# Three transformer layers behind a rotation: layers written out, w_up and the value columns converted elsewhere, setup transfers rearranged

## The chip, the cores and the metric

The kernel runs on one core of one Trainium2 chip. The metric is the device time of one execution in microseconds (us); less is better. All work is in fp32 accuracy: a matmul operand is split into a high part (fp32r) and a low part (the fp32 rest), and three products stand for one.

## The reference

Sixteen samples (B) of 256 tokens (T) with 288 channels (C). Layer 0 rotates each sample in a 64-dimensional subspace: it takes U from a QR factorisation of P and a rotation R = expm(A(cond)) per sample. Three layers follow, each with its own weights, modulated by the condition:

```python
z = einsum('btn,nd->btd', x, U)
x = x + einsum('btd,nd->btn', einsum('btd,bde->bte', z, R) - z, U)
for each of three layers:
    shift_a, scale_a, gate_a, shift_f, scale_f, gate_f = split(silu(cond) @ W_ada + b_ada, 6)
    h = layernorm(x) * (1 + scale_a) + shift_a
    q, k, v = h @ W_qkv + b_qkv            # 16 heads of 18
    x = x + gate_a * (softmax(q @ k.T / sqrt(18)) @ v @ W_proj + b_proj)
    h = layernorm(x) * (1 + scale_f) + shift_f
    x = x + gate_f * (gelu(h @ W_fc1 + b_fc1) @ W_fc2 + b_fc2)   # hidden size 1152
```

## The kernel before

`prepare` is the setup: rotation, modulation, and the first sample's queries, keys and values. The block of `layers` follows it behind a barrier of all engines. There each engine runs its own program, written out by hand in order and tied to the others by semaphores only. A program is a `prologue`, 48 half steps (`half_step(l, b)`: layer l, sample b, `it` = 16 l + b) and an `epilogue`. A half step works on three samples at once: attention of sample `it`, projection and MLP of sample `it - 1`, and queries, keys, values and first scores of `it + 1`.

TensorE goes, in a half step, through: projection of `it - 1` (two halves), the transposes of the maxima, then qk tile groups 0, 1, 2 of `it + 1` with shifted score units 0 to 2 between them, unit 3, the MLP transposes, unit 4, weighted values, units 5 and 6, values of `it + 1`, unit 7, `up` 0 to 4 with values between, score units of `it + 1` and `down`. Score units 5 to 7 need the b transfers of `stacks`.

`whole_run` (line 1492) sets the loops: half step (0, 0), then a loop over l = 0, 1 in the instruction stream that holds half step 1, an inner loop over b = 2 to 13, half steps 14, 15 and (l + 1, 0), and behind it a second copy for the last layer. So the code of a half step exists 10 times, and one jump leads back from (1, 0) to half step 1.

Weights come from DRAM in pieces and are converted: ACT or DVE copies the high part, POOL or DVE subtracts it to get the low part.
- w_up has two raw pieces of 128 x 1152 and three of 384 columns through staging. ACT makes the high parts (`high_weights`), POOL the low ones (`low_weights`, L1645): the first raw piece at the end of half step 0, the rest at the start of half step 1.
- w_in's query and key columns are converted by DVE in half step 14 (B-2), its value columns by DVE in half step 15 (B-1), behind the attention norm (`convert_weights`, L2264 and L2269). TensorE's `values` wait for them (`weights_ready`).
- `mlp_low` (POOL, L1636), `mlp_high` (DVE, L2242 to 2245), x_hat (DVE, L2230) and qk_low (DVE, L2253) are in every half step.

On ACT, `negate_maxima` (L1819) turns the transposed maxima into neg_max; ACT and SP each carry half of it into q_stack, and shifted unit 0 waits for both. `load_sums` waits for the store of the softmax sums and stands between gelu 0 and gelu 1.

SP issues most transfers in order: in the setup twelve query transfers (`query_stack`), then in the block of layers ten stores of rotated samples (L1538), a wait for the first keys, a signal to TensorE for score unit 5 (L1540), a wait for the stores (L1542), and `negated_maxima(0)`. In a half step: w_down's load (half step 1), x_mid, gates, x_in, `stacks` with 24 transfers, and in half step 0 the load of w_up's raw pieces behind them.

## Time and profile before

| what | value |
|---|---|
| median of 3 runs | 2068.33 us (2067.29 to 2071.01) |
| profiled execution | 2067.53 us, span 2065.8 us |
| TensorE busy (matmuls) | 1956.7 us, 95% |
| DVE, ACT, POOL busy | 1204.7, 1122.2, 1005.8 us (58, 54, 49%) |
| granted clock of TensorE, mean | 0.977 |
| start of the block of layers, first scores | 155.4, 156.8 us |
| mean half step from 300 us on | about 38 to 39 us |

The difference between the profiled execution's time and its span, 1.7 us, lies around the span. A granted clock of 1.0 is 2.4 GHz and 0.5 is 1.2 GHz. PE is TensorE's matmuls, PEld its weight loads. In a timeline row the bracket gives the idle time before the instruction and what ended it; "issue" means that the engine waited for nothing that the profile shows. In a row of waits the three numbers are the total, how many there were, and the longest.

### The profile page before, as it was taken

What the parts mean: (1) busy time and instruction counts of PE and PEld (TensorE: products, weight loads), DVE (VectorE), ACT (ScalarE), POOL (GpSimd) and SP (SyncE); (2) the same over time, 40 slices, a digit from 0 to 9 for tenths busy, and PEclk for the clock granted to TensorE, in tenths of its full rate; (3) what the DMA queues carried; (4) which work ended last, traced back from release to release, by engine and by line L of the source; (5) the groups of instructions that cost most, each with busy time, mean ns of one, the idle gap of its engine ahead of it and who ended that gap; (6) DMA issues with size and microseconds to landing.
All of it is one profiled execution on the core that took longest, in us unless ns stands there. A gap on an engine that the chain in (4) does not pass through costs nothing. (4 is left out here: it accounts for less than half of the span.)

```text
span 2065.8 us, 49808 instructions
## 1 busy us (share of the span) xinstructions
PE 1956.7 (95%) x16599; PEld 1748.2 (85%) x16599; DVE 1204.7 (58%) x2656; ACT 1122.2 (54%) x1929; POOL 1005.8 (49%) x1034
## 2 busy tenths in 40 slices
PE   6786999999999989899999999999899999999996
PEld 3554889989989979798999999988798999999986
DVE  7884655655546565655654655674665554654641
ACT  5333466465565556456556566455546556556452
POOL 1003645545545436554555544645564554544534
PEclk9997999999999999999999999999999999999998
DMA  8625433233333333433333333233433333333220
GB/s 220 136 72 162 118 107 98 83 102 91 92 95 87 99 89 112 142 92 94 89 95 98 81 105 98 83 103 95 138 82 103 91 92 95 87 101 99 76 80 26
DMA packets 138403, 207.01 MB, mean 100 GB/s; under 512 B 35688, under 2 KB 95686, under 8 KB 137254
## 3 DMA queue, kind: packets, MB, share of 16 engines
q1 hardware_dynamic: 110226, 168.27, 29.6%
q10 hardware_dynamic: 25460, 29.78, 5.2%
q0 software_dynamic: 2624, 7.77, 1.4%
q8 instruction: 53, 0.87, 0.2%
q14 instruction: 40, 0.33, 0.1%
HBM read 99.18 MB, written 20.82 MB: 58 GB/s over the span
## 5 line engine op out<-in xcount | busy, mean ns | idle before, releaser
L2277 DVE TENSOR_REDUCE maxima<-scores 128x4 f32<-128x1024 f32 x384 | 460.8, 1223 | 177.6 <-PE scores L2032 170.9
L1636 POOL TENSOR_TENSOR hidden<-g_full,hidden 128x512 fp32r<-128x512 f32 (+1 forms) x240 | 280.9, 1178 | 354.1 <-ACT hidden L1872 353.0
L1829 ACT ACTIVATE probs<-scores 128x1024 f32<-128x1024 f32 x384 | 383.3, 1027 | 94.6 <-PE pv_ps L2069 55.2
L2094 PE MATMUL mlp_ps<-h_mlp,w_up 128*128 128x256 f32 (+1 forms) x3024 | 406.3, 287 | 6.9 <-POOL h_mlp L1636 4.0
L2094 PEld LDWEIGHTS mlp_ps<-h_mlp,w_up 128*128 128x128 f32 (+1 forms) x3024 | 379.4, 191 | 36.4 <-issue 20.0
L1957 PE MATMUL mlp_ps<-w_down,hidden 128*128 128x288 f32 x2592 | 390.8, 296 | 0.0
L1957 PEld LDWEIGHTS mlp_ps<-w_down,hidden 128*128 128x128 f32 x2592 | 370.0, 189 | 18.6
L2032 PE MATMUL scores<-k_stack,q_stack 108*128 108x512 f32 x768 | 240.9, 406 | 17.5 <-DMA k_stack<-qk 7.1
L2055 PE MATMUL scores<-q_stack,k_stack 110*128 110x256 f32 x1536 | 246.9, 294 | 3.2 <-ACT probs L1829 2.0
L2055 PEld LDWEIGHTS scores<-q_stack,k_stack 110*128 110x128 f32 x1536 | 209.2, 192 | 31.8 <-issue 19.3
L1819 ACT ACTIVATE neg_max<-att_ps 16x256 fp32r<-16x256 f32 x48 | 18.0, 374 | 372.8 <-PE att_ps L2042 372.8
L1706 POOL TENSOR_TENSOR o_full<-o_full,inv_sum 128x512 f32<-128x512 f32 x96 | 139.7, 1474 | 157.5 <-DVE o_att L2289 157.5
L2282 DVE RECIPROCAL inv_few<-sums 128x32 f32<-128x32 f32 x48 | 17.0, 353 | 318.3 <-DMA sums<-sum_scratch 318.3
L1871 ACT ACTIVATE g_full<-mlp_ps 128x512 f32<-128x512 f32 (+1 forms) x240 | 133.7, 557 | 122.9 <-PE mlp_ps L2094 60.4
L1636 POOL TENSOR_TENSOR h_mlp<-h_full,h_mlp 128x512 fp32r<-128x512 f32 x48 | 72.5, 1511 | 260.3 <-DVE h_mlp L2243 260.2
L2069 PE MATMUL pv_ps<-probs,v_sb 128*32 128x256 f32 x3072 | 188.1, 385 | 0.6 <-ACT probs L1829 0.6
L1957 PE MATMUL mlp_ps<-w_out,o_att 128*128 128x288 f32 x1152 | 174.4, 302 | 5.4 <-issue 4.6
L1957 PEld LDWEIGHTS mlp_ps<-w_out,o_att 128*128 128x128 f32 x1152 | 160.6, 193 | 7.2 <-issue 4.9
L2032 PEld LDWEIGHTS scores<-k_stack,q_stack 108*128 108x128 f32 x768 | 129.0, 193 | 29.5 <-DVE maxima L2277 9.5
L2069 PEld LDWEIGHTS pv_ps<-probs,v_sb 128*32 128x32 f32 x3072 | 90.5, 110 | 65.3 <-issue 3.2
L2006 PE MATMUL att_ps<-h_att,w_in 128*126 128x256 f32 (+3 forms) x987 | 135.0, 284 | 1.6 <-DVE qk L2253 0.9
L1872 ACT ACTIVATE hidden<-mlp_ps 128x512 fp32r<-128x512 f32 (+1 forms) x240 | 132.1, 551 | 0.0
(265 smaller groups left out, 2819.7 us busy)
## 6 DMA issues: line engine op xcount, KB each, us to landing
q_stack<-qk SPq DMA_DIRECT2D x144, 180.0 KB
k_stack<-qk SPq DMA_DIRECT2D x282, 90.0 KB
inv_sum<-inv_scratch ACTq DMA_DIRECT2D x192, 128.0 KB, 2.7
k_stack<-qk SPq DMA_DIRECT2D x282, 54.0 KB
x_mid<-out_x SPq DMA_DIRECT2D x48, 288.0 KB, 4.2
out_x<-x_out SPq DMA_DIRECT2D x48, 288.0 KB, 3.1
x_in<-out_x SPq DMA_DIRECT2D x46, 288.0 KB, 3.9
q_stack<-qk SPq DMA_DIRECT2D x144, 72.0 KB
```

The lines of the kernel that those rows point to most:

```text
L1636: tt(out, full, high.bitcast(F32), ALU.subtract).then_inc(signal, 1)
L1706: tt(o_full[:, half, :], o_full[:, half, :], inv_sum[:, half, :], ALU.mult).then_inc(s_o_norm, 1)
L1829: evict(probs[:, u % 4, :, :, :], scores[u % 2][:, :, :, :], ACT.Exp, scale=SCALE)\
L1871: evict(g_full[:, n % 2, 0:width], bank[:, 0:width], ACT.Gelu_apprx_tanh).then_inc(s_gelu, 1)
L1872: evict(hidden[0][:, tiles, :].rearrange("p a t -> p (a t)"), bank[:, 0:width], ACT.Gelu_apprx_tanh)\
L1957: last = mm(out, a(left), c(weights[w]), start=start and n == 0, stop=stop and n == total - 1)
L2006: last = mm(qk_bank[n][0:cols.stop - cols.start, (m % 2) * T:(m % 2 + 1) * T], w[:, cols], h, start=count == 0, stop=count == 6)
L2032: last = mm(scores[u % 2][:, qt, :, :], q_stack[r, u, qt * P:(qt + 1) * P], k_stack[r, u, :, :], start=True, stop=True)
L2055: last = mm(scores[u % 2][:, par, kt, :], k_stack[r, u, par, kt * P:(kt + 1) * P], q_stack[r, u, :], start=True, stop=True)
L2069: last = mm(pv_ps[32 * i:32 * i + 32, (g % 2) * T:(g % 2 + 1) * T], v_sb[:, kt, 4 * g + i, :], probs[:, u % 4, i % 2, kt, :], start=kt == ...
L2094: last = mm(up_bank[n % 2][:, (m % 2) * T:(m % 2 + 1) * T], w[:, m * P:(m + 1) * P], h, start=count == 0, stop=count == 6)
L2277: nc.vector.tensor_reduce(out=maxima[:, :, :, u], in_=scores[u % 2][:, :, :, :], axis=AX.X, op=ALU.max).then_inc(s_max, 1)
```

## The change

In `whole_run` the loop over the layers is written out by the host program; only the inner loop over b stays a loop of the engine. There are then 15 copies of a half step.

Conversions: all of w_up's high parts are made by ACT at the end of half step 0; the low parts by DVE, the first raw piece at the end of half step 0, the others in half step 1 behind `mlp_high`. For the value columns of w_in ACT makes the high part at the end of half step 14, DVE the low part in half step 15 behind `mlp_high`. POOL keeps w_out and issues the staging transfers once DVE has freed a slot. In half steps 0 and 1 `load_sums` goes behind gelu 1.

Setup: POOL transfers keys (0, .) of both parts, ACT keys (1, .) and part a of (2, .), SP part b of (2, .). SP takes over the gate stores of layer 2. Six of the query transfers ("apart", 18 KB each) move into the block of layers, ahead of the ten stores. The w_up load of layer 0 goes from half step 0 to SP's prologue, ahead of `negated_maxima(0)`. Sample 1's qk tile group 1 is made in the prologue, behind the first scores, by TensorE, ACT and DVE.

```diff
--- before.py
+++ after.py
@@ prepare (setup): key transfers and gate stores
-        KEYS_OF_POOL, KEYS_OF_SCALAR = early["keys_of_pool"], ((2, 0), (2, 1))
+        KEYS_OF_POOL, KEYS_OF_SCALAR, KEYS_OF_SYNC = ((0, 0), (0, 1)), ((1, 0), (1, 1), (2, 0), (2, 1)), ((2, 0), (2, 1))
...
             early["query_stack"](sp, "a")
-            early["query_stack"](sp, "b")
+            early["query_stack"](sp, "b", "pairs")
+            for j, par in KEYS_OF_SYNC:
+                early["key_stack"](sp, "b", j, par)
+            store_gates(sp, slice(2, 3))
             sp.wait_ge(s_gates_st, 2 * 16 * TILES)
...
                 early["key_stack"](pool, "a", j, par, early["s_first_keys"])
+            for j, par in KEYS_OF_POOL:
+                early["key_stack"](pool, "b", j, par, early["s_first_keys"])
             pool.wait_ge(early["s_first_keys"], 64)
...
             for j, par in KEYS_OF_SCALAR:
-                early["key_stack"](act, "b", j, par)
+                if (j, par) not in KEYS_OF_SYNC:
+                    early["key_stack"](act, "b", j, par)
             mods_out(2)
-            store_gates(act, slice(2, 3))
...
             values(1)
+            differences(4)
             modulation_rows(2)
-            differences(4)
+            differences(5)
             modulation_columns(2)
-            for n in range(5, NPAIR):
+            for n in range(6, NPAIR):
                 differences(n)
@@ whole_run: the layers written out
-            with engine.Fori(0, L - 1) as l:
+            for l in range(L):
                 half_step(l, 1)
                 with engine.Fori(2, B - 2) as b:
                     half_step(l, b)
                 half_step(l, B - 2)
                 half_step(l, B - 1)
-                half_step(l + 1, 0)
-            half_step(L - 1, 1)
-            with engine.Fori(2, B - 2) as b:
-                half_step(L - 1, b)
-            half_step(L - 1, B - 2)
-            half_step(L - 1, B - 1)
+                if l < L - 1:
+                    half_step(l + 1, 0)
@@ sync
-            sp.sem_inc(s_stack_a, 64)
+            sp.sem_inc(s_stack_a, 32)
+            sp.sem_inc(s_stack_b, 32)
+            query_stack(sp, "b", "apart")
             for n in range(STORED, B):
                 sp.dma_start(dram["out"][n], x_all[:, n, :, :]).then_inc(s_out_st, 16)
-            sp.wait_ge(s_first_keys, 128)
-            sp.sem_inc(s_stack_b, 64)
             sp.wait_ge(s_out_st, 16 * B)
...
             def prologue():
+                raw_weights("w_up", up_raw[:, :, :], 0, s_up, PRE, 0)
                 negated_maxima(0)
...
-                if at(b, 0):
+                if at(b, 0) and before:
                     raw_weights("w_up", up_raw[:, :, :], l, s_up, UP_USES * it + PRE, 0)
@@ gpsimd
             def prologue():
-                for j, par in KEYS_OF_POOL:
-                    key_stack(pool, "b", j, par, s_first_keys)
...
-                if at(b, 1):
-                    low_weights("w_up_raw", l, (1,))
-                    low_weights("w_up", l, last_layer=last_layer)
                 if before:
                     mlp_low(it - 1)
                 if after_next:
                     inverse_deviation(0, it + 2)
+                if at(b, 1):
+                    stage_behind(l, OF["w_up"][0:1], "up", last_layer)
...
                 if at(b, 1):
+                    stage_behind(l, OF["w_up"][1:], "up", last_layer)
                     stage_behind(l, OF["b_down"], "down", last_layer)
...
                     add_mlp(it - 1, 1)
-                if at(b, 0):
-                    low_weights("w_up_raw", l, (0,))
@@ scalar
                 high_weights("w_out", 0)
                 load_table(ACT.Exp)
+                qk_high(1, 1)
...
                 negate_maxima(it)
-                if at(b, 1):
-                    high_weights("w_up_raw", l, (1,))
-                    high_weights("w_up", l)
                 for n in range(3):
-                    if after:
+                    if after and (before or n != 1):
                         qk_high(it + 1, n)
...
                     gelu(it - 1, 0)
-                load_sums(it)
+                late = at(b, 0) or at(b, 1)
+                if not late:
+                    load_sums(it)
                 if before:
                     gelu(it - 1, 1)
+                if late:
+                    load_sums(it)
...
                 if at(b, 0):
-                    high_weights("w_up_raw", l, (0,))
+                    high_weights("w_up_raw", l)
+                    high_weights("w_up", l)
+                if at(b, B - 2) and after_next:
+                    act.wait_ge(s_v_ps, 2 * (it + 1) + 2 + PRE)
+                    high_weights("w_in", l + 1, "v")
@@ tensor
                 pe.wait_ge(s_init, 5)
+                qk_tiles(1, 1, m_between=False)
...
                 for n in range(3):
-                    if after:
+                    if after and (before or n != 1):
                         qk_tiles(it + 1, n, m_between=before)
                     shifted_unit(it, n)
...
-                        weights_ready("w_up", l)
+                        weights_ready("w_up", l, "up")
@@ vector
+            def low_weights(l, which, part=None):
+                for n in which:
+                    dve.wait_ge(s_w_high, converted(n, l - 1 if part == "v" else l))
+                    dve.sem_inc(s_v_high, 1)
+                    for high, low_part, full in conversion(n, pieces[n]["low_rows"], part):
+                        last = tt(low_part, full, high.bitcast(F32), ALU.subtract)
+                    last.then_inc(s_v_low, 1)
...
                 for u in range(8):
                     unit_max(0, u)
+                qk_low(1, 1)
...
                     mlp_high(it - 1)
+                if at(b, 1):
+                    low_weights(l, UP_PIECES[1:])
+                if at(b, B - 1) and after:
+                    low_weights(l + 1, OF["w_in"], "v")
                 if after_next:
                     attention_norm(it + 2)
...
-                if at(b, B - 1) and after:
-                    dve.wait_ge(s_v_ps, 2 * it + 2 + PRE)
-                    convert_weights(l + 1, OF["w_in"], "v")
                 inverse(it)
...
                     gate_down(it - 1, 1)
+                if at(b, 0):
+                    low_weights(l, UP_PIECES[0:1])
```

## Rows read from the trace of the kernel before

**Rows 1.** Waits of TensorE, whole span: total us, times, longest us.
```profile
PE att_ps L2016 <- DVE w_in L2269: 9.7, 2, 4.9
PE mlp_ps L1965 <- DVE qk L2253: 7.6, 3, 3.6
PE mlp_ps L1957 <- issue: 4.6, 2, 2.3
PE mlp_ps L2094 <- ACT hidden L1872: 2.8, 5, 1.3
```

**Rows 2.** Windows of 10 us: window, length, busy by engine, PEclk (granted), DMA share, GB/s.
```profile
760.00:770.00 10.00, 5.15 (x26) 4.95 (x27) 4.53 (x15) 3.70 (x6) 2.44 (x3) 0.69 0.39 104
1470.00:1480.00 10.00, 7.19 (x61) 5.11 (x62) 7.89 (x21) 3.42 (x5) 6.43 (x8) 0.83 0.41 128
```

**Rows 3.** Timeline, TensorE, end of layer 0: start, us, instruction, idle before.
```profile
723.16 1.84 PE L2094 MATMUL mlp_ps<-h_mlp,w_up 128*128 128x256 f32 x14
765.95 2.05 PE L2016 MATMUL att_ps<-w_in,h_att 128*128 128x288 f32 x7 [4.85 <-DVE w_in L2269]
768.65 2.70 PE L2094 MATMUL mlp_ps<-h_mlp,w_up 128*128 128x256 f32 x14
```

**Rows 4.** Timeline, x_hat of half step 0 and 1 of layer 1, w_up on POOL.
```profile
799.35 1.21 DVE L2230 TENSOR_SCALAR x_hat<-x_one,mean_var,rstd 128x288 f32<-128x288 f32 x4 [0.37 <-POOL rstd L1633]
844.74 4.06 DVE L2230 TENSOR_SCALAR x_hat<-x_one,mean_var,rstd 128x288 f32<-128x288 f32 x4
844.37 2.66 POOL L1645 TENSOR_TENSOR w_up<-w_up_raw,w_up 128x1152 fp32r<-128x1152 f32 x1
```

**Rows 5.** Timeline, DVE in half steps 14 and 15 of layer 0, POOL's mlp_low.
```profile
720.58 0.42 DVE L2245 TENSOR_TENSOR h_mlp<-h_full,h_mlp 32x256 fp32r<-32x256 f32 x1
759.97 0.41 DVE L2245 TENSOR_TENSOR h_mlp<-h_full,h_mlp 32x256 fp32r<-32x256 f32 x1
764.59 1.30 DVE L2269 TENSOR_TENSOR w_in<-staging,w_in 128x288 fp32r<-128x288 f32 x3
760.02 1.52 POOL L1636 TENSOR_TENSOR h_mlp<-h_full,h_mlp 128x512 fp32r<-128x512 f32 x1 [5.99 <-DVE h_mlp L2243]
```

**Rows 6.** One line's instructions: duration ns min/median/max.
```profile
L2269 DVE TENSOR_TENSOR b_down<-staging,b_down x3: 448/1427/1434, 237.9 to 1490.9; 1x288 fp32r<-1x288 f32 x3
```

**Rows 7.** Timeline, TensorE, twelve projection matmuls usually and behind the jump.
```profile
748.78 1.84 PE L1957 MATMUL mlp_ps<-w_out,o_att 128*128 128x288 f32 x12
837.74 3.23 PE L1957 MATMUL mlp_ps<-w_out,o_att 128*128 128x288 f32 x12
```

**Rows 8.** Timeline, ACT, first raw half of w_up, layer 1.
```profile
830.38 1.16 ACT L1772 ACTIVATE w_up<-w_up_raw 128x1152 fp32r<-128x1152 f32 x1 [5.70 <-DMA w_up_raw<-in_w_up]
```

**Rows 9.** Timeline, last half step: ACT's neg_max, first shifted scores.
```profile
1997.27 0.37 ACT L1819 ACTIVATE neg_max<-att_ps 16x256 fp32r<-16x256 f32 x1 [10.70 <-PE att_ps L2042]
2000.04 1.21 PE L2055 MATMUL scores<-q_stack,k_stack 110*128 110x256 f32 x8 [1.22 <-DMA q_stack<-neg_max]
```

**Rows 10.** Timeline, TensorE, first sample: scores unit 5, shifted scores, next unit 5.
```profile
165.79 2.07 PE L2032 MATMUL scores<-k_stack,q_stack 108*128 108x512 f32 x4 [2.27 <-SPq L1540]
175.28 1.06 PE L2055 MATMUL scores<-q_stack,k_stack 110*128 110x256 f32 x4
203.79 2.07 PE L2032 MATMUL scores<-k_stack,q_stack 108*128 108x512 f32 x4 [5.85 <-DMA k_stack<-qk]
```

**Rows 11.** SP's stores and wait; DMA issues: KB, us to landing (last: window 213 to 217).
```profile
155.58 9.42 SPq L1538 DMA_DIRECT2D out_x<-w_rot_x  x10
SPq L1542 <- DMA out_x<-w_rot_x: 5.2, 1, 5.2
gate_a<-gate_scratch SPq DMA_DIRECT2D x48, 144.0 KB, 4.0
w_up_raw<-in_w_up SPq DMA_DIRECT2D x3, 1152.0 KB, 5.3
gate_a<-gate_scratch SPq DMA_DIRECT2D x1, 144.0 KB, 6.2
```

More of the change, by code:

```diff
@@ L1391, in query_stack @@
                     continue
[L1392 to L1393 removed]
+                if part != "apart":
+                    into_stack(engine, q_stack, tile, slice(2 * PAIR, 3 * PAIR), slice(0, 2), slice(first, first + PAIR), slice(5, 7),
+                               s_stack_b)
+                for par in range(2 if part != "pairs" else 0):
                     into_stack(engine, q_stack, tile, slice(3 * PAIR, 3 * PAIR + HD), slice(par, par + 1),
@@ L1763, in _, with high_weights @@
             evict = nc.scalar.activation
-            def high_weights(name, l, which=None):
-                for n in OF[name] if which is None else [OF[name][k] for k in which]:
+            def high_weights(name, l, part=None):
+                for n in OF[name]:
                     if n < NP:
@@ L1770, in high_weights @@
                         act.wait_ge(s_raw, 32 * l + 16)
-                    for high, _, full in conversion(n, slice(0, pieces[n]["rows"])):
+                    for high, _, full in conversion(n, slice(0, pieces[n]["rows"]), part):
                         last = evict(high, full, ACT.Copy)
@@ L2343, in half_step @@
                 if after:
-                    qk_low(it + 1, 1)
+                    if before:
+                        qk_low(it + 1, 1)
                     qk_low(it + 1, 2)
```

60 lines of the change are left out of this document (31 added, 29 removed).

## Prediction

> **What bounds the kernel now.** I read the wait totals of TensorE first [rows 1]. It is busy 95% of the span, and most half steps have no idle time at all: it is the bound, at full clock, so whatever the change does to the other engines is worth nothing there. What can be won is TensorE's idle time and the stretches at the lower clock, and these lie in four places: the end of a layer (waits for the value columns of w_in, 9.7 us in 2), half step 1 of each layer (waits for DVE's qk, 7.6 us in 3, and for ACT's late gelu), two waits, 4.6 us together, for which the profile names nothing, and the setup. The tail behind 1985 us is not touched. Then I read the engines' timelines around these places.
>
> **End of a layer, half step B-1, twice.** TensorE wants the value columns at 761.10 (765.95 less 4.85) and gets them at 765.95 [rows 3]. The window's granted clock is 0.69 [rows 2]: after the idle time the clock is at 1.2 GHz. The seven matmuls take 2.05 us there, the fourteen of up 2.70 against 1.84 [rows 3]; with those between them I count 2.2 us lost to the clock. So each layer end costs 7.05 us. The change takes the conversion out of the place behind the attention norm. The high part goes to ACT at the end of half step B-2 (three activations of 288 columns, a quarter of the 1152 that take 1.16 [rows 8], so about 1 us with their overheads, in an idle stretch before its next neg_max), the low part to DVE straight behind mlp_high. DVE is free at 760.38 (759.97 plus 0.41) and the three subtractions take 1.30 [rows 5]: 761.7, a wait of 0.6. But POOL has its own subtraction (mlp_low) from 760.02 to 761.54 [rows 5], and in this trace DVE and POOL operations over SBUF block each other: x_hat's four operations take 4.06 us while POOL converts w_up and 1.21 elsewhere [rows 4], and a 1x288 subtraction of DVE, on b_down, takes 448 ns at the least and 1434 at the most [rows 6]. That is the row nearest to the new subtractions, so I take it: DVE starts at 761.54, is done at 762.85, and TensorE waits 1.8. Bounds: 0.6 to 1.8 left. I take it that so short a wait leaves the clock up; a rival prices the other case. Gain 2 x (7.05 - 1.8) = 10.5 us.
>
> The Trainium skill says of this, in "SBUF — State Buffer", section "Who interferes with whom", that a DVE instruction with two SBUF inputs contends with a GpSimd instruction that reads SBUF, and that issue order decides who blocks. It speaks against these places for the subtractions, which have two SBUF inputs, and would leave 1.8 where an undisturbed DVE leaves 0.6. The rows on x_hat and on the 1x288 subtraction agree.
>
> **The jump of the layer loop, once.** Between layers 0 and 1 all engines go back to the top of the loop over l. There TensorE idles twice inside its projection, 4.6 us put down to "issue": it waited for nothing that the profile shows [rows 1]. The 12 matmuls behind it take 3.23 us against 1.84 [rows 7], and I put what their neighbours lose at another 1.3. Written out, this path has no jump; the other pass, from layer 1 to 2, falls through in the kernel before and has no such wait. Gain 4.6 + 2.7 = 7.3. The inner loops jump 12 times a layer without a gap, and stay.
>
> **Half step 1 of each layer, three times.** Before, POOL's subtractions for w_up run beside DVE's x_hat and hold it for 3 us [rows 4]; qk_low behind it comes late, and the MLP transposes wait: 7.6 us in 3 [rows 1]. Behind the longest one the clock falls (granted 0.83 over ten us, 1.7 us lost) [rows 2], and I count as much behind the second: 3.4. Moving the load of the sums behind gelu 1 frees the longest of the waits for gelu, 1.3 [rows 1], at 865 in half step 1 of layer 1. Away go 7.6 + 3.4 + 1.3 = 12.3. Two waits below 1 us at the same places I leave out.
> Back come two waits. First, all of w_up's high part is now on ACT at the end of half step 0, ahead of negate_maxima. For layers 1 and 2 the raw half of w_up lands only at 830.38, just as the next half step starts; two activations of 1.16 us [rows 8] and three of a third of their columns, which I put at 1.3 together, keep ACT to about 833.9. Without the jump neg_max would be due near 832.5, the shifted scores follow it by 2.77 [rows 9] and have about 0.2 to spare. That makes waits of 1.3 and, in layer 2, where the load lands 0.5 us later against the half step, about 2.0: 3.3 together (0 if the load came earlier). In layer 0 the load is in the setup, so nothing. Second, up(0) now waits for four DVE subtractions behind mlp_high: by the 1.30 us of three times 288 columns [rows 5] about 1.35 for the raw half's 1152 and 3 x 0.45 for the pieces of 384, 2.7, behind 1.16 us of POOL's mlp_low; up(0) is due 2.15 us after mlp_high (723.16 against 721.00) [rows 3, 5]. Wait 1.7, three times: 5.1 (bounds 1.5 to 5.1). Net 12.3 - 8.4 = 3.9. Queued behind the subtractions on DVE are the attention norm, w_down's conversion and the inverse of the sums; The inverse waits for the sums' transfer there in any case, so they stay hidden. The first raw piece, on DVE behind gate_down, delays the gating by up to 1 us, hidden by the second projection half. POOL's staging transfers for later pieces move back by some us and are needed later still.
>
> **Setup.** Before, unit 5 of the first scores waits 2.27 us for SP, which signals only behind ten stores [rows 10]. Now six small query transfers go ahead of these stores and nothing waits: -2.3. SP's last setup work becomes the four gate stores, whose landing the barrier awaits: +1.2 (bounds 0 to 2.5). The group of 14 matmuls beside the first scores runs at the lower clock (about 3.3 us) ahead of the maxima's transposes, filling a 1.4 us gap: neg_max comes about 0.8 us later than before. Then comes SP's queue: it waits for the stores (issued to 165.0, waited on for 5.2: 170.2) [rows 11], with the six transfers ahead of them about 171, and then issues the w_up load (5.3 us to landing) [rows 11] in front of SP's half of the negated maxima. A gate load issued behind such a large load took 6.2 us to land, against the usual 4.0, which ends it after the large one [rows 11]. So the maxima land near 176.5 and the shifted scores start near 177.2 instead of 175.28 [rows 10]. One qk group less is then between them, and ACT's exponentials end 0.5 us later than before. The wait of 5.85 for the keys at 203.79 [rows 10] follows from SP's 24 transfers behind them, and stays. Net +0.5, bounds -4 to +3.
>
> **Sum.** The profiled execution took 2067.5 us, 0.8 below the median of 2068.3. 10.5 + 7.3 + 3.9 - 0.5 = 21.2 less: 2046.3. With the waits left out I say 2046.
>
> **The rivals.**
> DVE isn't blocked. The five new subtraction runs each save 1.15: 2040. For it: the 448 ns case exists, and DVE may come first. Against: at a layer's end POOL's operation starts 0.36 us before DVE is free [rows 5]. 0.20.
> The setup wins. If the small maxima transfer overtakes the big load and the barrier doesn't move, 3.5 us less: 2042. Against it the gate row. 0.12.
> The clock falls behind the new waits. Seven places (two layer ends, two neg_max, three up) at 1.7: 12 us more, 2058. For it: the lower clock of [rows 2] stands behind waits of 3.6 us and more, and two short waits follow each other in one half step here; against: none of the new ones is over 2 us. 0.13.
> The change doesn't do what it says: the code after the layer's end is fetched anew anyway and the 7.3 us stay. 2053. Against it the fall-through into layer 2. 0.06.
> Slower: written out, there are 15 copies of the half step for 10. If the first pass through a copy cost what the jump cost, five more copies cost 36 us: 2082; it decides from four such stalls on. Against it: the copies passed first at 210 to 300 and at each layer's end show no such wait. 0.03. The Trainium skill, "Runtime: NRT & Kernel Launch", section "Instruction fetch mechanics", sets apart a taken branch, which forces a fetch, from straight code, whose fetch is mostly hidden; by that this rival falls.
>
> **How the numbers follow.** Forecast 0.45, rivals as above, and 0.01 for less than 4 us gained by any other way. A measurement tells about 0.2%, 4 us. Faster 0.95, same 0.02, slower 0.03. The range takes in all but the slower rival and the far half of the clock's: 2036 to 2056.
>
> **What would show it.** Right: no wait for w_in over 2 us near 761 and 1387; no "issue" wait near 831; x_hat in half step 1 at 1.2 us; waits of 1 to 2 us of the shifted scores for neg_max in layers 1 and 2, and of up(0) for DVE's w_up; the first shifted scores later than the first maxima by more than 3 us, with the w_up load landing in between. Wrong: DVE subtractions of 1152 columns at 1.3 us beside POOL's, a lower clock behind short waits, or "issue" waits in new places.

## The result and the profile after

The changed kernel takes 2044.07 us (2042.82 to 2044.86) against 2067.81 us (2066.25 to 2071.01) beside it: ratio 0.9881, 95% interval 0.9867 to 0.9894, 23.7 us less. The forecast was 2046, range 2036 to 2056. Its profiled execution has a span of 2041.8 us, 24.0 less than before.

The waits of TensorE after (engine, tile, line, what was waited for: us in total, times, longest), the rows that answer to [rows 1]. MLP transposes waiting for DVE's qk and the waits without a releaser inside the projection are no longer among them. The wait for the value columns of w_in has fallen from 9.7 to 2.4 us (first row). The others are new or have grown:

```profile
PE att_ps L2033 <- DVE w_in L2296: 2.4, 2, 1.2
PE mlp_ps L2120 <- ACT hidden L1884: 9.4, 11, 2.3
PE scores L2049 <- DMA k_stack<-qk: 8.9, 5, 5.5
PE scores L2072 <- DMA q_stack<-neg_max: 6.6, 4, 3.4
PE mlp_ps L2111 <- DVE w_up L2296: 4.2, 3, 1.5
```

TensorE's own timeline (start us, us, engine line operation, in brackets the idle time before and its releaser) shows where. In order: first shifted scores and the keys' wait in the setup; the layer end that answers to [rows 3]; half step 0 of layers 1 and 2; up(0) of half step 1 in the three layers:

```profile
176.56 2.08 PE L2072 MATMUL scores<-q_stack,k_stack 110*128 110x256 f32 x8 [3.43 <-DMA q_stack<-neg_max]
204.39 2.07 PE L2049 MATMUL scores<-k_stack,q_stack 108*128 108x512 f32 x4 [5.55 <-DMA k_stack<-qk]
225.98 1.93 PE L2111 MATMUL mlp_ps<-h_mlp,w_up 128*128 128x256 f32 x14 [1.35 <-DVE w_up L2296]
759.52 1.20 PE L2033 MATMUL att_ps<-w_in,h_att 128*128 128x288 f32 x7 [1.19 <-DVE w_in L2296]
813.10 0.40 PE L2120 MATMUL mlp_ps<-b_down,ones_l 128*128 128x288 f32 x1 [1.28 <-ACT hidden L1884]
840.39 1.93 PE L2111 MATMUL mlp_ps<-h_mlp,w_up 128*128 128x256 f32 x14 [1.50 <-DVE w_up L2296]
1373.50 1.21 PE L2033 MATMUL att_ps<-w_in,h_att 128*128 128x288 f32 x7 [1.19 <-DVE w_in L2296]
1428.02 0.40 PE L2120 MATMUL mlp_ps<-b_down,ones_l 128*128 128x288 f32 x1 [2.26 <-ACT hidden L1884]
1456.71 1.93 PE L2111 MATMUL mlp_ps<-h_mlp,w_up 128*128 128x256 f32 x14 [1.34 <-DVE w_up L2296]
```

A ledger tells where the 24 us came from better than any single wait. TensorE transposes the maxima once in each half step, so the distance from one such transpose to the next is the half step's length, free of everything that happens earlier. Undisturbed ones take 37.76 us in both kernels. These differ, (l,b) being half step b of layer l; all others together change by 0.3 us:

| half step | before, us | after, us | change |
|---|---|---|---|
| setup up to the first maxima | 170.91 | 170.08 | -0.8 |
| (0,0) | 39.32 | 40.67 | +1.3 |
| (0,1) and (0,2) | 44.86, 38.51 | 41.30, 37.77 | -4.3 |
| (0,15) | 45.17 | 41.22 | -3.9 |
| (1,0) | 43.65 | 39.18 | -4.5 |
| (1,1) and (1,2) | 45.61, 38.33 | 41.46, 39.02 | -3.5 |
| (1,14) and (2,14) | 38.04, 38.04 | 38.78, 38.78 | +1.5 |
| (1,15) | 46.83 | 39.94 | -6.9 |
| (2,0) | 38.13 | 41.71 | +3.6 |
| (2,1) and (2,2) | 45.41, 37.75 | 40.44, 37.82 | -4.9 |
| behind the last maxima | 68.95 | 67.64 | -1.3 |

The 1.3 us at the end are nobody's work: the same matmuls of the last scores run at a granted clock of 0.79 before and 1.00 after. The windows (length, busy us and count of each engine, granted clock, DMA share), first of before, then of after:

```profile
2001.89:2009.85 7.96, 7.14 (x59) 5.51 (x59) 3.70 (x10) 4.93 (x6) 1.84 (x2) 0.79 0.20 57
```

```profile
1979.19:1985.94 6.75, 5.83 (x58) 4.16 (x59) 3.70 (x10) 4.82 (x6) 1.86 (x2) 1.00 0.22 72
```

How far may a half step be trusted? The changed kernel, run once more (k11_after_again), gives all half steps within 0.5 us of the table except (1,2) and (1,14), which are 1.1 us shorter: waits of around 1 us for a transfer come and go there. The +1.5 of half steps 14 are thus partly chance; (2,0) was 41.72 again. The part behind the last maxima was not the same: 71.8 us in place of 67.6, with the last projection taking 4.97 us instead of 3.45 behind a wait of 2.42 us instead of 1.14. So the 1.3 us gained there in the table are chance, and that second execution has a span of 2044.1 us, 21.7 less than before instead of 24.0.

The kernels of the experiments below tell more, in places that their edits don't touch. The nine executions with the changed setup and its order of transfers (all but k3_maxima_first and k10_together) end half step (0,0) anywhere from 209.5 to 212.1 us. Four kernels have a wait of 1.5 to 1.9 us for the keys in half step (0,1) or (1,1), which is then 0.8 to 3.1 us longer than in the changed kernel. Between two single executions a difference below about 1 us in a half step, or 2 us in the setup, may be chance, if no wait of the trace goes with it.

### The profile page after: what moved, and what is told of

The parts are those of the page before. It is cut to its first block and busy times, and to the rows that moved or that the text cites. A ratio compares the mean times of both kernels' runs of the same rounds, so it can differ in the third digit from the quotient of the medians.

```text
span 2041.8 us, 48800 instructions
## 1 busy us (share of the span) xinstructions
PE 1944.5 (95%) x16599; PEld 1738.8 (85%) x16599; DVE 1213.3 (59%) x2665; ACT 1124.3 (55%) x1935; POOL 987.5 (48%) x1015
## 5 line engine op out<-in xcount | busy, mean ns | idle before, releaser
L1653 POOL TENSOR_TENSOR hidden<-g_full,hidden 128x512 fp32r<-128x512 f32 (+1 forms) x240 | 286.7, 1204 | 326.8 <-ACT hidden L1884 326.1
L2111 PE MATMUL mlp_ps<-h_mlp,w_up 128*128 128x256 f32 (+1 forms) x3024 | 402.1, 286 | 8.8 <-DVE w_up L2296 4.2
L2072 PEld LDWEIGHTS scores<-q_stack,k_stack 110*128 110x128 f32 x1536 | 207.3, 190 | 38.1 <-issue 19.8
```

The source lines that it names most:

```text
L1653: tt(out, full, high.bitcast(F32), ALU.subtract).then_inc(signal, 1)
L2072: last = mm(scores[u % 2][:, par, kt, :], k_stack[r, u, par, kt * P:(kt + 1) * P], q_stack[r, u, :], start=True, stop=True)
L2111: last = mm(up_bank[n % 2][:, (m % 2) * T:(m % 2 + 1) * T], w[:, m * P:(m + 1) * P], h, start=count == 0, stop=count == 6)
```

## Experiments

By their medians and intervals the edits of k2_late_b1, k3_maxima_first, k5_pool_behind, k6_pv_first and k9_spread_last can't be told from the changed kernel one by one. What is said of them rests on the half steps and waits of their profiled executions.

**The jump alone.** The kernel before with one edit.

```diff
-            with engine.Fori(0, L - 1) as l:
+            for l in range(L):
                 half_step(l, 1)
...
-                half_step(l + 1, 0)
-            half_step(L - 1, 1)
...
+                if l < L - 1:
+                    half_step(l + 1, 0)
```

> The kernel before with one edit: the loop over the layers is written out. Theory (the jump's cost is the jump's alone): the 4.6 us of waits with no releaser at 832.86 and 836.30 and the slow matmuls behind them go, 7.3 us in all: 2067.8 - 7.3 = 2060.5. Half step (1,0), from its maxima transposes to the next ones, falls from 43.65 us to the 37.8 of an undisturbed one, and the other half steps keep theirs. Rival 1 (the code behind a layer's end is fetched anew in any case): no change, 2067.8, the two waits stay. Rival 2 (each copy passed for the first time costs a fetch): waits without a releaser appear in new places, 2072 and up.

Measured: 2059.66 us against 2065.69, ratio 0.9966 (0.9953 to 0.9978): 6.0 us less by the medians, 7.0 by the ratio (4.5 to 9.7). No wait without a releaser is left near the place. (1,0) falls by 4.0 and (1,1), which held the slow matmuls behind the second wait, by 1.0. But (1,0) ends at 39.69, not 37.8, and (2,0), which had no jump, grows from 38.13 to 39.85. The whole agrees with the jump's forecast price. The ledger is less kind: at the place itself 5.0 us go and 1.7 come back in (2,0). The rest of the 6.7 us between the two profiled executions lies in half steps that the edit should leave alone, such as (2,1) with -1.7 and (1,15) with -2.1, or (0,15) with +1.3. Something small comes with the written-out code.

**The loop over the layers back in the changed kernel.** The same edit the other way round.

> The changed kernel with the loop over the layers back, all else kept. Theory (the parts add up): two waits without a releaser, 4.6 us, return in the projection of half step (1,1), with 2.7 us of slow matmuls: 2044.1 + 7.3 = 2051.4. Rival (the jump was paid for by something that the moved conversions also remove, so it costs nothing or half now): 2044 to 2048. Half step (1,0) goes from 39.18 us to 45 by the theory.

Measured: 2051.92 us, ratio 0.9925 (0.9898 to 0.9951), the 2051.4 of the theory. The waits are back:

```profile
828.98 1.32 PE L1981 MATMUL mlp_ps<-w_out,o_att 128*128 128x288 f32 x8 [2.45 <-issue]
832.30 1.33 PE L1981 MATMUL mlp_ps<-w_out,o_att 128*128 128x288 f32 x4 [2.01 <-issue]
```

and (1,0) takes 44.89 us, 5.7 more, and (1,1) 45.12, 3.7 more. The other side of the same trade: (2,0) falls from 41.71 to 38.08. There the wait shows up that I had forecast and that the changed kernel doesn't have. ACT (first fence) is busy with w_up until neg_max, and TensorE (second fence) waits 0.70 us for neg_max and 0.37 for its transfer:

```profile
1449.08 2.22 ACT L1788 ACTIVATE w_up<-w_up_raw 128x1152 fp32r<-128x1152 f32 x2 [5.93 <-DMA w_up_raw<-in_w_up]
1451.20 1.33 ACT L1788 ACTIVATE w_up<-staging 98x384 fp32r<-98x384 f32 x3
1452.44 0.36 ACT L1835 ACTIVATE neg_max<-att_ps 16x256 fp32r<-16x256 f32 x1
```

```profile
1452.94 1.89 PE L2027 MATMUL att_ps<-h_att,w_in 128*126 128x256 f32 x14 [0.70 <-ACT neg_max L1835]
1455.20 0.74 PE L2076 MATMUL scores<-q_stack,k_stack 110*128 110x256 f32 x4 [0.37 <-DMA q_stack<-neg_max]
```

**POOL or DVE for w_up's low parts.** In the changed kernel POOL does them again, in front of mlp_low in half step 1; the high parts stay on ACT at the end of half step 0.

```diff
-        BY_POOL = [*OF["w_out"]]
+        BY_POOL = [*OF["w_out"], *UP_PIECES]
...
                 if at(b, 1):
-                    stage_behind(l, OF["w_up"][0:1], "up", last_layer)
+                    low_weights("w_up_raw", l)
+                    low_weights("w_up", l, True)
+                    stage_up(l, last_layer)
...
-                if at(b, 1):
-                    low_weights(l, UP_PIECES[1:])
```

The third argument has POOL wait for each of its own pieces before the next.

> The changed kernel with one part undone: the low parts of w_up are computed by POOL again, in half step 1 of each layer in front of mlp_low, all five together; the high parts stay where the change puts them. Theory (POOL's subtractions block DVE's x_hat, and this is what the move to DVE removes): x_hat's four operations in half step 1 go from 1.22 us to 4 or more, the MLP transposes wait 1.7 to 3.6 us for DVE's qk again, the granted clock of these half steps falls from 1.00 to 0.95 or 0.96, and the waits of up(0) for DVE go. Half steps (l,1) go from 41.1 to about 45 us, 3 x 4 more: 2056. Rival (the gain in these half steps comes from the high parts, which no longer hold ACT up behind neg_max): half steps (l,1) keep 41 us or fall to 39.8, as the 1.4 us waits of up(0) go: 2040 to 2044.

Measured: 2056.51 us, ratio 0.9951 (0.9931 to 0.9970): the 2056 of the theory. Half steps (l,1) take 46.1, 44.8 and 45.3 us. DVE, then POOL, then TensorE in (1,1), the row on DVE being the one that answers to [rows 4]:

```profile
833.21 6.45 DVE L2259 TENSOR_SCALAR x_hat<-x_one,mean_var,rstd 128x288 f32<-128x288 f32 x4 [0.55 <-POOL rstd L1650]
```

```profile
833.04 5.32 POOL L1659 TENSOR_TENSOR w_up<-w_up_raw,w_up 128x1152 fp32r<-128x1152 f32 x2
838.44 3.33 POOL L1659 TENSOR_TENSOR w_up<-staging,w_up 33x384 fp32r<-33x384 f32 x3
```

```profile
840.40 1.16 PE L1996 MATMUL mlp_ps<-ident,x_hat 128*128 128x128 f32 x6 [4.07 <-DVE qk L2282]
```

The single operations behind these rows show how. DVE's first x_hat operation starts 0.17 us behind POOL's first subtraction and ends 0.17 us behind its end; the second likewise beside POOL's second subtraction, 2.6 us for 0.3 to 0.4 of work. The third takes 0.42 us, the fourth 0.98 beside POOL's first piece of 384 columns. So one operation of DVE gets through between two of POOL, and each next one is held again. The high parts on ACT are not what helped: they are the same in this kernel. The Trainium skill says in "SBUF — State Buffer", section "Who interferes with whom", that for a DVE instruction in its two-port mode, which tensor_scalar can enter, the engine that issued first has the shared pair for the whole instruction and the other fully blocks. No run shows which mode x_hat ran in; POOL started first here by 0.17 us, and in the order of the two ends the trace agrees.

**POOL behind DVE at a layer's end.** In the changed kernel POOL's mlp_low of half step B-1 waits until DVE's three subtractions for the value columns are done.

```diff
+                if at(b, B - 1) and after:
+                    n = OF["w_in"].stop - 1
+                    pool.wait_ge(s_v_low, converted_by_vector(n, "v", l + 1))
                 if before:
                     mlp_low(it - 1)
```

> The changed kernel, but at a layer's end (half step B-1) POOL's mlp_low waits until DVE has done its three subtractions for the value columns of w_in. In the changed kernel these take 2.29 us (757.17 to 759.46) beside mlp_low (756.78 to 758.30), and TensorE waits 1.19 us for them. Theory (POOL's operation holds DVE's subtractions up): alone they take 1.30 us, the wait falls to 0.2, and both layer-end half steps shorten by 1.0 us each, unless up(0) then waits for the later mlp_low (due at about 760.0, which mlp_low just reaches). 2044 - 2 = 2042. Rival (the subtractions are slow by themselves here, by their strided columns): they take 2.29 still, the wait of TensorE stays at 1.2 and a new one for mlp_low comes behind it: 2045.

DVE in the changed kernel, then in this one, then POOL in this one:

```profile
757.17 2.29 DVE L2296 TENSOR_TENSOR w_in<-staging,w_in 128x288 fp32r<-128x288 f32 x3
```

```profile
758.71 1.31 DVE L2299 TENSOR_TENSOR w_in<-staging,w_in 128x288 fp32r<-128x288 f32 x3
```

```profile
760.10 1.29 POOL L1653 TENSOR_TENSOR h_mlp<-h_full,h_mlp 128x512 fp32r<-128x512 f32 x1 [8.17 <-DVE w_in L2299]
```

The subtractions take 1.31 us, no wait for w_in of 0.3 us or more is left at either layer end, none for mlp_low comes, and (0,15) and (1,15) shorten by 1.1 and 0.9. The whole, 2041.49 us, ratio 0.9870 (0.9847 to 0.9893), can't tell 2 us by itself; the two half steps do. The same 2.29 and 1.31 us in one place, with POOL's operation moved and nothing else, is the cleanest measure here of what the two engines cost each other.

**Work in front of the wait.** In the changed kernel, in half step 1, TensorE does weighted_values of group 2 before up(0).

```diff
                     if at(b, 1):
+                        weighted_values(it, 2)
                         weights_ready("w_up", l, "up")
                     up(m, 0)
-                weighted_values(it, 2)
+                if not at(b, 1):
+                    weighted_values(it, 2)
```

> The changed kernel, but in half step 1 of a layer TensorE does weighted_values of group 2 in front of up(0), not behind it. Theory: the waits of 1.35, 1.50 and 1.34 us for DVE's w_up at up(0) come from subtractions that can't be earlier; 0.96 us of work in front of them takes as much off each: waits of 0.4 to 0.5 are left, half steps (l,1) shorten by 0.95 each, 2044 - 2.9 = 2041. Rival (what follows up(0), ACT's gelu behind its copies, is what bounds the half step): the idle time moves to a later wait for ACT's hidden, no gain, 2044.

Measured: 2040.87 us, ratio 0.9866 (0.9843 to 0.9889). The waits of up(0) fall to 0.37, 0.34 and 0.48 us, as the theory says, and new waits of 1.0 to 1.1 us appear at the last group of up, as the rival says:

```profile
838.40 1.93 PE L2111 MATMUL mlp_ps<-h_mlp,w_up 128*128 128x256 f32 x14 [0.34 <-DVE w_up L2298]
849.03 1.11 PE L2111 MATMUL mlp_ps<-h_mlp,w_up 128*128 128x256 f32 x7 [1.09 <-ACT hidden L1884]
```

(0,1) and (1,1) shorten by 0.5 and 0.9, (2,1) takes 40.60 instead of 40.45: under half of the expected gain.

**The maxima in front of the big load.** In the changed kernel's setup SP sends its half of the negated maxima first.

```diff
             def prologue():
-                raw_weights("w_up", up_raw[:, :, :], 0, s_up, PRE, 0)
                 negated_maxima(0)
+                raw_weights("w_up", up_raw[:, :, :], 0, s_up, PRE, 0)
```

> The changed kernel, but in the setup SP sends its half of the negated maxima before the load of w_up's raw half, not behind it. Theory: the wait of 3.43 us of the first shifted scores at 176.56 comes from the load in front of the maxima; it falls to below 0.8, and all behind it comes 2.7 us or more earlier: 2041.3. The 5.55 us wait for the keys at 204.39 stays as long as it is, since SP's transfers for it start from the same scores. Rival 1 (the maxima are late for another reason, the queries' apart transfers or the stores): the wait stays, 2044. Rival 2 (the gain is given back at the keys, the wait there grows to 8): 2044, with the first shifted scores at 173.9.

SP's queue in the changed kernel, then in this one, then TensorE in this one:

```profile
170.39 0.34 SPq L1592 DMA_DIRECT2D w_up_raw<-in_w_up  x1
171.23 0.69 SPq L1585 DMA_DIRECT2D q_stack<-neg_max  x1
```

```profile
172.31 0.68 SPq L1585 DMA_DIRECT2D q_stack<-neg_max  x1
173.18 0.56 SPq L1592 DMA_DIRECT2D w_up_raw<-in_w_up  x1
```

```profile
174.60 1.22 PE L2072 MATMUL scores<-q_stack,k_stack 110*128 110x256 f32 x8 [0.40 <-DMA q_stack<-neg_max]
201.24 2.07 PE L2049 MATMUL scores<-k_stack,q_stack 108*128 108x512 f32 x4 [5.95 <-DMA k_stack<-qk]
```

From SP's issue of the maxima to the shifted scores it is 5.3 us behind the load (176.56 less 171.23) and 2.3 us in front of it. (0,0) falls from 40.67 to 36.50, the wait for the keys grows by 0.4, and the first maxima come 1.1 us later, so that (0,1) begins 3.1 us earlier. (0,1) itself is 1.1 us longer than in the changed kernel, with a wait of 1.49 us for the keys. 2040.25 us, ratio 0.9866 (0.9842 to 0.9890).

**Half step 0 of a layer.** Two edits of one kind. The first has the late load of the sums in half step 1 only; the second also puts all spreading transfers behind gelu 4 in half step 0.

```diff
-                late = at(b, 0) or at(b, 1)
+                late = at(b, 1)
```

```diff
-                        if n == 3:
+                        if n == (UP_USES - 1 if at(b, 0) else 3):
                             spread_inverse(it, (0, 1))
```

> The changed kernel, but the load of the sums stays in front of gelu 1 in half step 0 of a layer and is behind it in half step 1 alone. In the changed kernel TensorE waits 1.28 and 2.26 us for ACT's hidden at 813.10 and 1428.02, in half steps (1,0) and (2,0), and never for neg_max in half step 1 of layers 1 and 2. Theory (one wait covers the other): without the late load the two waits go, and TensorE then comes to its shifted scores in half steps (1,1) and (2,1) before neg_max has landed, since ACT still converts w_up until 825.2: waits of about 0.8 and 1.8 us for neg_max there. Half steps (1,0) and (2,0) lose 3.5 together, (1,1) and (2,1) gain 2.6: 2043. Rival (the load order alone costs the 3.5, and nothing was covered): the 3.5 us are gained whole, 2040.5. Rival 2 (the waits at 813 and 1428 come from something else, as the jump's absence): they stay, 2044.

> The changed kernel with two edits in half step 0 of a layer alone: the load of the sums in front of gelu 1, and all four transfers that spread the inverse behind gelu 4. Theory (the last gelu waits for the landing of the inverse, behind which ACT issues its spreading): the waits for ACT's hidden in front of the down product (1.28 and 2.26 us) go in both half steps; a wait of about 1.1 for the first gelus in (1,0) stays, as the sums' store lands in 3.3 us there. (2,0) falls from 41.7 to below 39, (1,0) stays at 39: 2041. If the waits of half step 0 covered a late neg_max, as I forecast it, then half step (2,1) grows by 1 us, since ACT's w_up pieces end 39.3 us after the start of half step (2,0) and neg_max is then due after 38.2: 2042. Rival (the late inverse is wanted by DVE's normalise just behind): the wait moves to a later engine, (2,0) keeps 41: 2044.

The first: 2042.20 us, ratio 0.9869 (0.9844 to 0.9894). (2,0) falls to 39.54, (1,0) stays at 39.22, since in place of the wait in front of down one of 1.13 us for the second gelu comes. (1,1) and (2,1) change by less than 0.3, and neg_max is waited for in neither. The theory that the one wait covers the other had no chance to show: ACT's w_up pieces end 39.3 us after the start of (2,0), and neg_max is due 0.4 us after its end, so it would be late only behind a half step shorter than 38.9 us. The loop-back kernel above has one, and shows it. The second: 2040.62 us, ratio 0.9874 (0.9858 to 0.9891). The waits in front of down are gone, but waits of 1.04 and 1.05 us for earlier gelus, and in (2,0) one of 0.60 for DVE's maxima, take their place: (1,0) 39.79, (2,0) 40.23. Neither does better than the other; the wait moves among the neighbours. The second has (0,1) at 44.44 us, 3.1 more than the changed kernel, with a wait of 1.94 us for the keys at 249.45 and a granted clock of 0.83 in the ten us behind it.

What made (2,0) long in the changed kernel? TensorE waits for the last gelu, and ACT, before that gelu, for the store of the inverse to land. ACT's queue there, and what the DMA view shows of the first 1.5 us behind the store (1423.16 to 1424.66):

```profile
1423.16 0.34 ACTq L1864 DMA_DIRECT2D inv_scratch<-inv_few  x1
1426.38 0.84 ACTq L1870 DMA_DIRECT2D inv_sum<-inv_scratch  x2
```

```profile
q8 instruction: 1, 0.02, 5.0%
```

The spreading follows the store after 3.22 us. That is not the work of the late load alone. ACT issues the load of the sums 21.1 us into the half step in the changed kernel and 21.0 with the first edit, since in both it waits for the sums' own store. With the late load kept, the kernel with the loop back and the one with more code written out (below) have 1.49 us from store to spreading in (2,0) and take 38.08 and 39.58 us; the first edit has 1.89 and takes 39.54. None of these three has an instruction packet that starts in the first 1.5 us behind the store. So the first edit's gain in (2,0) can't be put down to the order of the load; the section on the hardware has the count over all traces.

**More code passed once.** In the changed kernel layer 1's inner loop is written out, 12 copies of the half step in place of one.

```diff
-                with engine.Fori(2, B - 2) as b:
-                    half_step(l, b)
+                if l == 1:
+                    for b in range(2, B - 2):
+                        half_step(l, b)
+                else:
+                    with engine.Fori(2, B - 2) as b:
+                        half_step(l, b)
```

> The changed kernel with layer 1's inner loop written out as well: 12 copies of the half step in place of a loop of 12 passes; the order of all work is the same. Theory (code that runs straight on costs nothing, nor do the inner loop's jumps): each half step keeps its 37.8 us, 2044. Rival (a copy passed for the first time costs what the jump of the layer loop cost, or a part): waits without a releaser in each of the 12, 1 to 7 us each: 2056 to 2128.

Measured: 2046.26 us, ratio 0.9904 (0.9879 to 0.9928), 2 us above the changed kernel and within both intervals. Behind the setup no wait without a releaser appears. But half steps (1,2) to (1,13) take 457.8 us, against 454.6 in the changed kernel and 453.1 for twelve undisturbed ones: 0.4 us a copy against the undisturbed ones, in lumps of 0.4 to 1.3 us in six of them. The other six take 37.65 to 37.71 us, 0.1 less than a pass of the loop. The profiled execution as a whole is 2.2 us shorter than the changed kernel's, as (0,15), (1,1), (1,14) and (2,0) came out 1.1 to 2.1 us shorter: the price of writing out is read from the copies, and no total shows it. In (1,11), 39.08 us long, the transfer of the inverse lands late. ACT's queue in this kernel (the store of the inverse, then the first of its spreading transfers, which waits for the store to land), and in the changed kernel in the same half step:

```profile
1228.37 0.35 ACTq L1868 DMA_DIRECT2D inv_scratch<-inv_few  x1
1231.55 0.80 ACTq L1874 DMA_DIRECT2D inv_sum<-inv_scratch  x2
```

```profile
1229.84 0.35 ACTq L1864 DMA_DIRECT2D inv_scratch<-inv_few  x1
1231.43 0.81 ACTq L1870 DMA_DIRECT2D inv_sum<-inv_scratch  x2
```

3.18 us instead of 1.59. What differs in the DMA view of that half step (queue, kind: packets, MB, share) is that instructions are fetched; of the changed kernel's loop passes (1,3) to (1,12) none shows such packets:

```profile
q8 instruction: 2, 0.03, 0.4%
q14 instruction: 2, 0.02, 0.1%
```

**The changed kernel again, and four edits together.** Both ran on one chip with the spreading kernel; the second has the edits of the maxima, of POOL behind DVE, of weighted_values and of the spreading.

> The changed kernel once more, beside the next two on the same chip: 2044.1, with half step (2,0) at 41.7 us and a wait of 2.3 us for ACT's hidden in it if that belongs to the kernel, at 38 to 40 if it was the chance of one execution.

> The edits of four experiments together in the changed kernel: SP's half of the negated maxima in front of the setup's w_up load (3.1 us), POOL's mlp_low behind DVE's subtractions at a layer's end (2.0), weighted_values in front of up(0) in half step 1 (1.4), and the sums' load and the spreading of the inverse as in the experiment before (2.5). If they add up: 2044.1 - 9 = 2035. Rival (the stages overlap, so that one's gain is another's wait): 2038 to 2041.

The changed kernel: 2044.63 us, ratio 0.9891 (0.9874 to 0.9907). The four together: 2037.63 us (2031.25 to 2041.99), ratio 0.9852 (0.9831 to 0.9873), the lowest median of all, 7 us below the changed kernel beside it, between the 2035 of the theory and the 2038 of the rival. (0,0) gains its 4.2, but (0,15) and (1,15) gain 0.5 and 0.7 only, and (1,1) is 2.6 us longer than in the changed kernel, with a wait of 1.88 us for the keys at 856.23 and a granted clock of 0.83 in the ten us behind it. Its two best edits are the ones that were measured in place: the order on SP in the setup, and POOL behind DVE.

## Why the prediction was right, point by point

The time came out 2 us from the forecast, and the terms at the layer's end, the jump and the setup hold. That it came so near is partly luck: the gain in half step 1 was 7.4 us larger than forecast, and 5.0 us that I had at nothing were lost in half step 0, 6.5 with half steps 14. With the first error alone the sum would have been 2039. In the ledger of the profiled executions, 21.2 us were forecast and 24.0 came, 21.7 in the second execution.

**Layer end: right.** Forecast 10.5, or 5.25 each; measured 10.8, but as 3.9 in (0,15) and 6.9 in (1,15). With the written-out kernel before as the base, which waits 4.5 us for w_in at both ends and takes 46.49 and 44.75 us, it is 5.3 and 4.8: the size holds, and the uneven parts are chance. The step that DVE is blocked by POOL's mlp_low is shown by k5_pool_behind, 2.29 against 1.31 us. The wait left was 1.19 instead of 1.8: TensorE came 1.2 us after DVE was free, not 0.7. The rival that DVE isn't blocked (2040) falls. A wait of 1.00 us for the maxima at 749.25 in the same half step was not forecast; it was 0.78 when the kernel ran again and 1.27 in the kernel before with its layers written out, so it can come without the moved conversions.

**Jump: right, in kind and in about its size.** Forecast 7.3. Taken from the kernel before it gives 6.0 by the medians and 7.0 by the ratio, put back into the changed one 7.8 and 9.1. In the half steps (1,0), (1,1) and (2,0) alone it is 3.3 us the first way and 5.8 the second, so the near agreement of the totals says less than it seems to. The two waits without a releaser are gone and come back with the loop, which is shown. The rival that its cost stays (2053) falls.

**Half step 1: mis-sized, too small.** Forecast 3.9 net. Half steps (l,1) and (l,2) gained 12.7, of which 1.4 are the jump's slow matmuls, so 11.3. The busy windows of TensorE split it. Before, the three half steps (l,1), then after:

```profile
210.23:255.09 44.86, 40.58 (x319) 35.77 (x318) 31.64 (x48) 24.07 (x40) 27.84 (x28) 0.96 0.45 132
837.46:883.07 45.61, 41.28 (x319) 36.75 (x318) 31.62 (x48) 24.19 (x40) 26.29 (x27) 0.95 0.45 136
1459.99:1505.40 45.41, 39.85 (x321) 35.04 (x319) 30.02 (x48) 24.43 (x41) 28.29 (x27) 0.96 0.37 109
```

```profile
210.75:252.05 41.30, 38.93 (x321) 34.48 (x319) 31.93 (x52) 21.79 (x36) 22.56 (x23) 1.00 0.49 142
825.03:866.49 41.46, 38.65 (x321) 34.54 (x319) 33.11 (x53) 22.08 (x37) 25.56 (x26) 1.00 0.50 149
1441.50:1481.94 40.44, 38.61 (x320) 34.44 (x318) 32.91 (x53) 21.79 (x36) 22.44 (x21) 1.00 0.41 123
```

Busy time falls by 5.5 us (121.7 to 116.2): the clock was below full in all three half steps, and I had counted it behind two waits; less the jump's share it gives 4.1 instead of 3.4. Idle time falls by 7.2 (14.2 to 7.0), where I had 8.9 going and 8.4 coming. Of that error of 6.7, 3.3 are the waits for neg_max, which didn't come; 0.9 is up(0), 4.2 instead of 5.1; the rest are waits of about 1 us and less that I left out on purpose or took for nothing. They were not small together: a place that is disturbed by 8 us has more than its named waits in it. The mechanism, POOL's subtractions holding x_hat, is shown by k7_up_by_pool. The working of the wait at up(0) holds too. DVE's subtraction of the first raw piece at the end of half step (0,0), with POOL idle, and of the second in (1,1) beside POOL's mlp_low, then POOL's:

```profile
209.33 1.35 DVE L2296 TENSOR_TENSOR w_up<-w_up_raw,w_up 128x1152 fp32r<-128x1152 f32 x1
836.47 2.34 DVE L2296 TENSOR_TENSOR w_up<-w_up_raw,w_up 128x1152 fp32r<-128x1152 f32 x1
```

```profile
836.07 1.52 POOL L1653 TENSOR_TENSOR h_mlp<-h_full,h_mlp 128x512 fp32r<-128x512 f32 x1 [5.05 <-DVE h_mlp L2261]
```

With the three small pieces DVE is done 3.9 us after mlp_high, as forecast (1.16 and 2.7); up(0) was due 2.5 us after it instead of 2.15, so the wait is 1.5 and not 1.7.

**Half step 0: the term that was missing.** I had nothing for (1,0) beside the jump, and nothing for (2,0). Measured: (1,0) keeps 1.4 of the jump's share of 5.9, and (2,0) grows by 3.6, with a granted clock of 0.96 in it behind its 2.26 us. The forecast wait for neg_max in half step 1 and this wait in half step 0 exclude each other. My margin of 0.2 us assumed that half step 0 would be an undisturbed one; longer by 1.4 and 3.9 us, it gives ACT the time to finish w_up before neg_max is due. In the kernel with the loop back, where (2,0) is undisturbed, 1.07 of my 2.0 us appear. So the wait was real in kind and about half of my size, and another wait, one half step earlier, stood in its place. What I missed in (2,0) is that the last gelu stands behind the landing of the inverse's store, and that this store lands late there: 3.2 to 3.9 us to the next transfer in the changed kernel, its repeat and the kernels k3_maxima_first, k5_pool_behind, k6_pv_first and k7_up_by_pool, which all have (2,0) at 41.7 to 42.4 us. Where it is 1.5 to 1.9 us, with the late load of the sums or without it, (2,0) takes 38.1 to 39.9. The slow cases go with an instruction fetch beside the store; that writing out the layers put one there fits the loop-back kernel (38.08), and is not shown further. What is left (39.5 to 39.9 against 38.1) comes with the written-out code too, since the kernel before, with nothing but its layers written out, has 39.85 and both kernels with the loop 38.1.

**Setup: right, by its path.** Forecast +0.5, measured +0.5. The agreement to the tenth is luck: the same setup ends (0,0) between 209.5 and 212.1 us in nine executions, the kernel before at 210.2. The maxima behind the big load held the scores until 176.56 (forecast 177.2), and k3_maxima_first shows the load as the cause. The barrier moved by 0.4, not 1.2.

**The clock's rival (2058)** falls for waits of 1.2 to 1.5 us: the three half steps (l,1) have 1.00 after. Behind 2.26 us it did fall, as behind the 3.6 us and more of [rows 2], and behind the waits of 1.94 and 1.88 us for the keys in two experiments (0.83 over ten us). Had the 1.8 us that I forecast at the layer's end come, and not 1.19, the rival would have been nearer. And the last scores of all had 0.79 and 1.00 behind the same 1.2 us wait, so near that length it is chance.

**The slower rival (2082)** falls in size, not in kind. I let it go for the reason that copies passed first show no such wait. They show none without a releaser; they show late transfers, 0.4 us a copy. The Trainium skill, "Runtime: NRT & Kernel Launch", section "Instruction fetch mechanics", calls the cost of crossing a block boundary in a long kernel mostly hidden; with no wait without a releaser and 0.4 us of 37.8 in the written-out layer the runs agree.

## What to carry to other kernels

Before pricing single waits, cut the span into periods by an instruction that comes once in each, compare each with an undisturbed one, and price the whole excess: it holds the small waits and the lower clock, which single waits leave out. When a new wait is forecast from a margin, ask what else lengthens the period in front of it, since two waits on one path don't add. Put an operation of POOL behind a short one of DVE rather than beside it when TensorE waits for DVE's, and a transfer that is waited for in front of a large one on its queue, not behind it. And run the changed kernel twice: the second execution here moved 4 us at the end that no edit had touched.

## What the runs showed of the hardware

Beside two subtractions of POOL over 128x1152 elements and a smaller one, four operations of DVE, which take 1.22 us alone, took 6.45 us, one of them getting through behind each of POOL's. A single one of POOL of 1.5 us cost DVE's three subtractions of 288 columns, and its one of 1152, 1.0 us each. It goes the other way too: at 1441.08 DVE's subtraction of 1152 columns starts 0.2 us before POOL's x_out and takes its 1.35 us, while x_out takes 1.79 instead of 0.81.

Writing out a loop can have a small price of its own. In the written-out layer 1 the spreading followed the store of the inverse after up to 3.18 us, instead of 1.50 to 1.68 in the changed kernel's loop passes, and in one copy, (1,9), ACT took 2.04 us to issue two transfers instead of 0.80. In each copy passed once some 3 to 6 instruction packets are seen, in the passes (1,3) to (1,12) of the inner loop none, and 11 in the half step with the jump of the outer loop, (1,0) of the loop-back kernel:

```profile
q8 instruction: 5, 0.08, 0.8%
q14 instruction: 6, 0.05, 0.4%
```

The 13 traces of this case hold 598 half steps ((0,1) to (2,14)) with this store and its successor. In 18 of them an instruction packet of 16 KB starts on queue 8 within 1.5 us behind the store: the spreading follows after 2.6 to 3.6 us in all 18. In 4 it is a packet on queue 14 alone: 2.0 to 2.6 us. In the 576 others the median is 1.6 us, and 5 are above 2.2: in four of these ACT issues the spreading only behind gelu 4, in the fifth the packet starts at 1.6 us. That the packets themselves delay the store is still argued from their coming together; no run moved a packet and nothing else. In half step 0 of layers 1 and 2 the load of the sums follows their store after 2.5 to 3.6 us in every kernel run here but the one before, which has 1.9 there, as all have in most loop passes; why it is late just there stays open.
